# Row sums of three narrow attentions taken from the value products, with masks and a partition shuffle to join the halves

## Chip, cores and metric

One core of one Trainium2 chip. The metric is the device time of one execution, in microseconds (us); the kernel is launched once.

## What is computed

Two layers on x of 8 batches x 256 tokens x 256 features, each a self-attention, a cross-attention and a feed-forward part, with a layer norm after each. Three of these parts are attentions with 16 heads of 16 features ("narrow"), and they alone are changed:

```python
# L0x: cross-attention to 77 context rows; q and k normalized per head, rotary embedding on q
attn = softmax(einsum('bhqd,bhkd->bhqk', q, k)); o = einsum('bhqk,bhkd->bhqd', attn, v)
# L1x: cross-attention to the same 77 rows, scale 0.25
# L1s: self-attention over 256 tokens inside the last part, after an rms norm
ctx = einsum('bhst,bthd->bshd', softmax(scores), v);  X = X + ctx @ wo
```

A softmax row is exp(s - max) divided by its row sum; the kernel divides after the product with the values.

## The kernel before

The program runs seven stages one after the other: L0a (attention with heads of 64), L0x, the expert choice, L1a, L1x, L1s, the mixture of experts. L0x and L1x come from `context_stage`, L1s from `narrow_stage`. Each engine runs its own list of instructions in a hand-written order; semaphores join them.

The three narrow stages have one shape. A batch b has four steps st, numbered through as n = 4b + st, 32 in all; a step covers four heads, one in each 32-row group of TensorE. For each step:

- TensorE computes scores (queries on partitions) in two pairs of heads into `psS`; VectorE takes the negative row maxima of each pair (`row_max`) into `top`; TensorE transposes them (item "top"), and VectorE adds them to the queries (`shift`).
- TensorE computes the turned products (keys on partitions, maxima already subtracted) in two halves into `psK`; ScalarE takes the exponentials of each half into `pT`. Each half of the turned products is issued beside scores of a later step (`turned_beside_scores`): half 0 of step n beside pair 1 of step n+1, half 1 beside pair 0 of step n+2.
- TensorE multiplies `pT` with the values (`values`, into `psO[:, 0:S]`) and with ones (`row_sums`, into `psO[:, S:2S]`). A head group has 32 columns, for two heads of 16: even and odd steps use the same group. In `vs` each pair of heads has four places of 16 columns: values, empty, empty, values. The even step multiplies with the first two, the odd one with the last two, so the empty columns (zeros) leave the other head's partitions of `psO` as they are; `ones` has ones in one half and zeros in the other, in the same way.
- After each odd step VectorE divides: `out_norm(o)`, o = n // 2, a reciprocal of the sums and a product. ScalarE (`out_high`) and GpSimd (`out_low`) split the result into two parts for the output product (item "out").

TensorE's order in the loop over n: turned half 0, items of slot (st, 0), values of step n-1, item "top" of n+1, turned half 1, row sums of n-1, items of slot (st, 1). Items are projections and transposes for the next batches (q, k, v, qk, xT, kT, qT) and the output product; each takes one of NF banks of `psF` (3 in L0x and L1x, 1 in L1s). A few items "top" in L0x and L1x are preceded by products whose result nobody reads (line 466, `keep_busy`): 1 in L0x at steps 0 and 2 at steps 2, 1 in L1x at steps 0 and, from batch 4 on, at steps 1.

VectorE's order: row_max(n+1, pair 1), what it takes of slot (st, 0), shift(n+1), row_max(n+2, pair 0), at even st `out_norm(n // 2 - 1)`, then other work (in L1s, at st 2, `spread` of the batch before; at st 1 `front_stats`; in L0x at st 2 `join_pairs`). `values` of an even step waits for `o_norm`, since it starts `psO` anew. GpSimd's order in L1s at st 1: `root_front(b+2)`, then `out_low`.

Of the kernel before, what the change touches and what calls it, by code (L numbers as in the profile page):

```python
# [11 lines left out]
F32 = mybir.dt.float32  # L12
# [23 lines left out]
EULER = 2.718281828459045  # L36

# [43 lines left out]
def make_constants(nc, ctx):  # L81
# [6 lines left out]
    sums = nc.dram_tensor("moe_sums", [B * S + P, D], F32).ap()  # L88
    zeroed = ctx.enter_context(nc.semaphore("const_zeroed"))
# [18 lines left out]
    return ident, ident_bf, mask_bf, blank, rows, sums, []  # L108


def context_stage(nc, name, kind, consts, x_in, x_out, w, gate_w=None, aff=None):
# [16 lines left out]
    with ExitStack() as ctx:  # L128
# [19 lines left out]
        ones = sb("ones", [P, 2, 2, HD])  # L148
        rinv = sb("rinv", [P, 2, S])
        oN = sb("oN", [P, 2, S])  # L150
# [58 lines left out]
        k_ready, p_exp = sem("k_ready"), sem("p_exp")  # L209
        r_ready, r_inverse, o_norm, o_high, o_low = sem("r_ready"), sem("r_inverse"), sem("o_norm"), sem("o_high"), sem("o_low")  # L210
# [144 lines left out]
        def _(pool):  # L355
# [100 lines left out]
        def _(pe):  # L456
# [165 lines left out]
            def values(n):  # L622
                b, st = divmod(n, NST)
                par = st % 2
                pe.wait_ge(p_exp, 2 * n + 2)
                if par == 0 and n >= 2:
                    pe.wait_ge(o_norm, n // 2)
                wait_taken(pe, ("v", b // 2), 0)
                for j in range(4):
                    pe.matmul(psO[32 * j:32 * j + 32, 0:S],  # L630
                              vs[0:CTX, b, 4 * (st // 2) + j, 2 * par:2 * par + 2, :].rearrange("p a e -> p (a e)"),
                              pT[0:CTX, n % 2, j, :], start=(par == 0), stop=False)

            def row_sums(n):
                par = n % 2
                if n == 0:
                    pe.wait_ge(zeroed, 5)
                for j in range(4):
                    last = pe.matmul(psO[32 * j:32 * j + 32, S:2 * S], ones[0:CTX, par, :, :].rearrange("p a e -> p (a e)"),
                                     pT[0:CTX, n % 2, j, :], start=False, stop=(par == 1))  # L640
                last.then_inc(r_ready, 1)
# [7 lines left out]
            for n in range(N):  # L649
# [9 lines left out]
                if n:  # L659
                    row_sums(n - 1)  # L660
# [3 lines left out]
            row_sums(N - 1)  # L664
# [6 lines left out]
        def _(act):  # L671
            def take(what, b):
# [42 lines left out]
                elif what[0] == "v":  # L715
                    if what[1] == 0:
                        act.wait_ge(zeroed, 3)
# [30 lines left out]
            def exponential(n, half):  # L748
# [3 lines left out]
                act.activation(pT[0:CTX, n % 2, 2 * half:2 * half + 2, :], psK[0:CTX, :, 0:S], ACT.Exp).then_inc(p_exp, 1)  # L752

# [35 lines left out]
            for n in range(N):  # L789
# [11 lines left out]
                if st == 1 and n // NST >= 2:  # L801
                    finish(n // NST - 2)
            out_high(N // 2 - 1)
# [6 lines left out]
        def _(dve):  # L810
# [102 lines left out]
            def row_max(n, pair):  # L913
# [3 lines left out]
                if n == 0:  # L917
                    dve.wait_ge(zeroed, 3)
# [150 lines left out]
def narrow_stage(nc, name, kind, consts, x_in, x_out, w, extra_out=None):  # L1069
# [16 lines left out]
    with ExitStack() as ctx:  # L1086
# [16 lines left out]
        ones = sb("ones", [P, 2, 2, HD])  # L1103
        rinv = sb("rinv", [P, 2, S])
        oN = sb("oN", [P, 2, S])
# [65 lines left out]
        k_ready, p_exp = sem("k_ready"), sem("p_exp")  # L1171
        r_ready, r_inverse, o_norm, o_high, o_low = sem("r_ready"), sem("r_inverse"), sem("o_norm"), sem("o_high"), sem("o_low")
# [112 lines left out]
        def _(pool):  # L1285
# [22 lines left out]
            pool.memset(vs[:, :, :, :, 1:3, :].rearrange("p r t h e d -> p (r t h) (e d)"), 0.0).then_inc(zeroed, 1)  # L1308
            pool.memset(ones[:], 0.0).then_inc(zeroed, 1)
            pool.wait_ge(zeroed, 3)  # L1310
            for r in range(2):
                pool.memset(ones[:, r, r, :], 1.0).then_inc(zeroed, 1)
# [82 lines left out]
        def _(pe):  # L1395
# [143 lines left out]
            def values(n):  # L1539
# [3 lines left out]
                if par == 0 and n >= 2:  # L1543
                    pe.wait_ge(o_norm, n // 2)
                wait_taken(pe, ("kv",) if rope else ("v",), b)
                for kt in range(KT):
                    for j in range(4):
                        h2 = 4 * (st // 2) + j
                        pe.matmul(psO[32 * j:32 * j + 32, 0:S],
                                  vs[0:KP, b % RV, kt, h2, 2 * par:2 * par + 2, :].rearrange("p a e -> p (a e)"),  # L1550
                                  pT[0:KP, n % 2, j, kt * S:(kt + 1) * S], start=(par + kt == 0), stop=False)

            def row_sums(n):
                par = n % 2
                if n == 0:
                    pe.wait_ge(zeroed, 5)
                for kt in range(KT):
                    for j in range(4):
                        last = pe.matmul(psO[32 * j:32 * j + 32, S:2 * S],
                                         ones[0:KP, par, :, :].rearrange("p a e -> p (a e)"),  # L1560
# [1982 lines left out]
```

## Time and profile before

| | us |
|---|---|
| median of 3 runs | 2167.03 (2165.86 to 2175.17) |
| profiled execution, its own time | 2174.54 |
| its span, first to last instruction | 2172.8 |
| TensorE matmul busy | 1866.4 (86%) |
| VectorE busy | 1202.6 (55%) |
| ScalarE busy | 995.1 (46%) |
| GpSimd busy | 677.5 (31%) |
| mean granted TensorE clock | 0.928 of full |

In order of time the stages lie at: L0x to 575 us, its loop from 383 to 557; L1x loop 1382 to 1534; L1s loop 1587 to 1819; the mixture of experts from 1834. Reading the rows: PE is TensorE's matmul, PEld its weight load, DVE VectorE, ACT ScalarE, POOL GpSimd. A name like L1x_psO is a tile of that stage. `[0.88 <-ACT ...]` at the end of a row of the order of time is the idle time of the engine before it and what is taken to have ended it. The granted clock is the share of the full 2.4 GHz that TensorE was given.

### The profile page before, as it was taken

To read this page: it belongs to the slowest core of one execution; us is meant where nothing else is said; L and a number is where in the kernel's file an instruction comes from. 1 tells how busy PE (TensorE), PEld (TensorE's weight loads), DVE (VectorE), ACT (ScalarE), POOL (GpSimd) and SP (SyncE) were. 2 spreads that over 40 slices of the span, in tenths; PEclk is the share of its full clock that TensorE was granted. 3 is DMA by queue.
4 is the path that set the end of the run, shared out by engine and by line. 5 is a ranking of instruction groups with operands and counts; after the bars stand their busy time and mean duration, and the time that the engine had idled before them with its cause. 6 is when DMAs were issued, how large, how long until landed. Compare 5 with 4: busy or idle time off the path is not lost. (4 is left out here: it accounts for less than half of the span.)

```text
span 2172.8 us, 41833 instructions
## 1 busy us (share of the span) xinstructions
PE 1866.4 (86%) x15764; PEld 1453.1 (67%) x15764; DVE 1202.6 (55%) x2996; ACT 995.1 (46%) x2350; POOL 677.5 (31%) x609
## 2 busy tenths in 40 slices
PE   7888875999489999399999995999599896999994
PEld 6676764676278898277777774666366564788884
DVE  3666654666535455245555554466456664447774
ACT  5656542443245454345555552444244342346663
POOL 2333334675332432223333333111101000243443
PEclk9999996998589999699999999899599997999997
DMA  2000002000353522610000001000103102823333
GB/s 65 11 11 21 11 11 71 2 31 11 114 163 107 155 81 46 202 38 1 11 21 11 11 6 44 26 24 18 56 1 109 50 12 94 308 99 52 52 52 100
DMA packets 97870, 125.52 MB, mean 58 GB/s; under 512 B 8554, under 2 KB 84794, under 8 KB 97642
## 3 DMA queue, kind: packets, MB, share of 16 engines
q1 hardware_dynamic: 84378, 105.07, 14.6%
q0 software_dynamic: 13296, 17.77, 4.8%
q8 instruction: 131, 2.15, 0.4%
q14 instruction: 65, 0.53, 0.1%
HBM read 85.02 MB, written 39.89 MB: 57 GB/s over the span
## 5 line engine op out<-in xcount | busy, mean ns | idle before, releaser
L2110 POOL TENSOR_TENSOR L1a_probs<-L1a_probs,L1a_rinv 128x1024 f32<-128x1024 f32 x64 | 121.3, 1895 | 269.2 <-DVE L1a_rinv L2424 269.2
L2107 POOL TENSOR_TENSOR L0a_probs<-L0a_probs,L0a_rinv 128x256 f32<-128x256 f32 (+1 forms) x128 | 103.3, 828 | 189.6 <-DVE L0a_rinv L2424 189.5
L2416 DVE CUSTOM_DVE_ANT_0 L1a_sbias<-L1a_psS,L1a_bias 128x256 f32<-128x256 f32 x256 | 93.2, 421 | 109.2 <-PE L1a_psS L2218 109.2
L2369 ACT ACTIVATE L1a_probs<-L1a_sbias,L1a_nmx 128x256 f32<-128x256 f32 x256 | 126.5, 497 | 40.0 <-DVE L1a_nmx L2416 40.0
L2369 ACT ACTIVATE L0a_probs<-L0a_sbias,L0a_nmx 128x128 f32<-128x128 f32 (+1 forms) x256 | 112.8, 443 | 29.8 <-DVE L0a_nmx L2416 29.8
L3082 POOL DMA_INDIRECT moe_sums<-moe_y,moe_xg x39 | 81.0, 2076 | 136.8 <-DVE moe_y L3381 117.9
L2667 POOL DMA_INDIRECT ec_sums<-ec_yk,ec_token_at x32 | 59.0, 1844 | 190.5 <-ACT ec_yk L2788 185.6
L1643 ACT ACTIVATE L1s_pT<-L1s_psK 128x1024 f32<-128x1024 f32 x64 | 65.6, 1025 | 102.7 <-PE L1s_psK L1516 102.7
L2853 DVE TENSOR_TENSOR ec_h<-ec_sg,ec_psU 128x512 f32<-128x512 f32 x64 | 44.0, 687 | 119.9 <-ACT ec_sg L2775 119.9
L1790 DVE TENSOR_REDUCE L1s_top<-L1s_psS 128x4 f32<-128x1024 f32 x64 | 78.4, 1226 | 48.4 <-PE L1s_psS L1501 48.3
L3160 PE MATMUL moe_psY<-moe_wts,moe_hT 128*128 (+1 forms) x440 | 104.0, 379 | 0.8 <-ACT moe_hT L3227 0.8
L2700 PE MATMUL ec_psG<-ec_xs,ec_wt 128*128 128x512 f32 x384 | 99.3, 394 | 2.1 <-issue 2.1
L2416 DVE CUSTOM_DVE_ANT_0 L0a_sbias<-L0a_psS,L0a_later 128x128 f32<-128x128 f32 (+1 forms) x256 | 76.1, 354 | 43.6 <-PE L0a_psS L2215 43.1
L2700 PE MATMUL ec_psU<-ec_xs,ec_wt 128*128 128x512 f32 x384 | 98.7, 393 | 0.0
L2714 PE MATMUL ec_psA<-ec_wdt,ec_hT 128*128 128x256 f32 x768 | 94.4, 284 | 0.2 <-DVE ec_hT L2812 0.2
L2714 PEld LDWEIGHTS ec_psA<-ec_wdt,ec_hT 128*128 128x128 f32 x768 | 92.8, 192 | 0.5 <-DVE ec_hT L2812 0.4
L3160 PEld LDWEIGHTS moe_psY<-moe_wts,moe_hT 128*128 128x128 f32 x440 | 83.1, 189 | 14.2 <-issue 1.0
L2431 DVE COPY L1a_pT<-L1a_psT 128x1024 f32<-128x1024 f32 x64 | 78.2, 1222 | 20.7 <-PE L1a_psT L2233 20.7
L2700 PEld LDWEIGHTS ec_psG<-ec_xs,ec_wt 128*128 128x128 f32 x384 | 72.7, 191 | 17.3 <-issue 2.4
L2247 PE MATMUL L0a_psO<-L0a_pT,L0a_lat 128*64 128x256 f32 (+1 forms) x512 | 56.9, 342 | 31.8 <-issue 31.6
L2775 ACT ACTIVATE ec_sg<-ec_psG 128x512 f32<-128x512 f32 x64 | 38.2, 597 | 99.1 <-PE ec_psU L2700 99.1
L2700 PEld LDWEIGHTS ec_psU<-ec_xs,ec_wt 128*128 128x128 f32 x384 | 72.9, 190 | 15.4
(527 smaller groups left out, 5016.1 us busy)
## 6 DMA issues: line engine op xcount, KB each, us to landing
ec_wg<-in_L_ffn_w_gate SPq DMA_DIRECT2D x8, 1024.0 KB, 9.4
ec_wu<-in_L_ffn_w_up SPq DMA_DIRECT2D x8, 1024.0 KB, 13.1
ec_wd<-in_L_ffn_w_down SPq DMA_DIRECT2D x8, 1024.0 KB, 6.2
moe_rows<-blank SPq DMA_DIRECT2D x1, 5070.0 KB, 19.2
moe_xg<-moe_rows SPq DMA_DIRECT2D x39, 130.0 KB, 2.1
moe_wts<-in_L_ffn_e_gate SPq DMA_DIRECT2D x8, 512.0 KB, 10.1
moe_wts<-in_L_ffn_e_up SPq DMA_DIRECT2D x8, 512.0 KB, 10.0
moe_wts<-in_L_ffn_e_down SPq DMA_DIRECT2D x8, 512.0 KB, 10.1
```

Of the source, the lines that this page charges most:

```text
L1643: act.activation(pT[0:KP, n % 2, 2 * half:2 * half + 2, :], psK[0:KP, :, 0:KT * S], ACT.Exp).then_inc(p_exp, 1)
L1790: dve.tensor_reduce(top[:, n % 2, :, 64 * pair + HD:64 * pair + 64:32].rearrange("p t j -> p j t"), psS[:, 2 * pair:2 * pair + 2, :].rearr ...
L2107: last = pool.tensor_tensor(v, v, bcast(rinv[:, r, :, t], 2, KEYS[t]), ALU.mult)
L2110: last = pool.tensor_tensor(v, v, bcast(rinv[:, r, :, :].rearrange("p h t -> p (h t)"), 2, S), ALU.mult)
L2369: ins = act.activation(probs[:, r, j, at], sbias[:, g % 2, j, at], ACT.Exp, bias=nmx[:, r, j, t:t + 1], scale=-1.0, accum_out=sums[:, r, j ...
L2416: last = dve.tensor_tensor_reduce(out=sbias[:, g % 2, j, at], in0=psS[:, slot + j, at], in1=added, scale=-1.0, scalar=LARGE, op0=ALU.add, ...
L2431: dve.tensor_copy(pT[:, g % 2, :, :].rearrange("p j (k r c) -> p r (j k) c", r=2, c=64), psT[:, :, 0:PW].rearrange("p r (n c) -> p r n c", ...
L2667: pool.indirect_dma_start(sums, bass.IndirectOffsetOnAxis(ap=token_at[:, s, e:e + 1], axis=0), yk[:, e % 2, s, :], None, compute_op=ALU.add)\
L2700: last = pe.matmul(ps[:, i % 2, :], wt[:, a, j, c, i * P:(i + 1) * P], xs[:, b, c, :], start=(n == 0), stop=(n == len(products) - 1))
L2714: last = pe.matmul(psA[:, half, s % 2 * D:(s % 2 + 1) * D], hT[:, a, i, s * P:(s + 1) * P], wdt[:, b, i, :], start=(i + n == 0), stop=(i = ...
L3082: pool.indirect_dma_start(sums, bass.IndirectOffsetOnAxis(ap=xg[:, j % RX, D:D + 1].bitcast(U32), axis=0), y[:, j % RY, :], None, compute_ ...
L3160: last = pe.matmul(psY[:, 0:D], hT[:, g % 2, f, :], down_weights(e)[:, f * D:(f + 1) * D], start=(f == 0), stop=(f == FC - 1))
```

## The change

`vs` gets ones instead of zeros in its empty columns, so the same product gives in one half of the 32 partitions the values and in the other half the row sums of that head. Since the even and the odd step now both fill all partitions, they go to different halves of `psO`: even to 0:S, odd to S:2S. `row_sums` and the tile `ones` go away. For the even step the values lie on the lower 16 partitions of each group, the sums on the upper 16; for the odd step it is the other way round. To join them, ScalarE copies `psO[:, 0:S]` twice (`out_halves`), with a mask of 0 and 1 per partition as scale (`which_half`), and VectorE adds the other half under the opposite mask. That gives all sums and all values, with the sums of a head 16 partitions away from its values; the reciprocal is taken and shuffled by 16 partitions within each group of 32 (`SWAPPED`). The masks are made once, on VectorE, from the identity matrix.

```diff
+SWAPPED = [*range(16, 32), *range(16)]
 # make_constants: after the GpSimd work
+            dve.wait_ge(made, 5)
+            dve.tensor_reduce(sixteens[:], ident[:].rearrange("p (a e) -> p a e", e=16), AX_X, ALU.add).then_inc(counted, 1)
+            dve.wait_ge(counted, 1)
+            dve.tensor_reduce(which_half[:], sixteens[:].rearrange("p (a h) -> p h a", h=2), AX_X, ALU.add).then_inc(counted, 1)
 # both stages, GpSimd
-            pool.memset(vs[:, :, :, 1:3, :], 0.0).then_inc(zeroed, 1)
-            pool.memset(ones[:], 0.0).then_inc(zeroed, 1)
-            pool.wait_ge(zeroed, 3)
-            for r in range(2):
-                pool.memset(ones[:, r, r, :], 1.0).then_inc(zeroed, 1)
+            pool.memset(vs[:, :, :, 1:3, :], 1.0).then_inc(zeroed, 1)
 # TensorE
                 if par == 0 and n >= 2:
-                    pe.wait_ge(o_norm, n // 2)
+                    pe.wait_ge(o_joined, n // 2)
-                    pe.matmul(psO[32 * j:32 * j + 32, 0:S],
+                    last = pe.matmul(psO[32 * j:32 * j + 32, par * S:(par + 1) * S],
...
-            def row_sums(n):
...
                 turned_beside_scores(n, 1)
-                if n:
-                    row_sums(n - 1)
 # ScalarE
+            def out_halves(o):
+                act.wait_ge(r_ready, 2 * o + 2)
+                if o >= 2:
+                    act.wait_ge(o_joined, o - 1)
+                act.activation(half_sums[:, o % 2, :], psO[:, 0:S], ACT.Copy, scale=which_half[:, 1:2])
+                act.activation(half_values[:, o % 2, :], psO[:, 0:S], ACT.Copy, scale=which_half[:, 0:1]).then_inc(o_halved, 1)
...
                 if st % 2 == 1 and n >= 3:
                     out_high(n // 2 - 1)
+                if st % 2 == 0 and n >= 2:
+                    out_halves(n // 2 - 1)
                 exponential(n, 1)
 # VectorE
             def out_norm(o):
-                dve.wait_ge(r_ready, 2 * o + 2)
-                dve.reciprocal(rinv[:, o % 2, :], psO[:, S:2 * S]).then_inc(r_inverse, 1)
-                dve.wait_ge(r_inverse, o + 1)
+                dve.wait_ge(o_halved, o + 1)
                 if o >= 2:
                     dve.wait_ge(o_low, o - 1)
-                dve.tensor_tensor(oN[:, o % 2, :], psO[:, 0:S], rinv[:, o % 2, :], ALU.mult).then_inc(o_norm, 1)
+                dve.scalar_tensor_tensor(out=all_sums[:, o % 2, :], in0=psO[:, S:2 * S], scalar=which_half[:, 0:1],
+                                         in1=half_sums[:, o % 2, :], op0=ALU.mult, op1=ALU.add).then_inc(o_joined_sums, 1)
+                dve.scalar_tensor_tensor(out=all_values[:, o % 2, :], in0=psO[:, S:2 * S], scalar=which_half[:, 1:2],
+                                         in1=half_values[:, o % 2, :], op0=ALU.mult, op1=ALU.add).then_inc(o_joined, 1)
+                dve.wait_ge(o_joined_sums, o + 1)
+                dve.reciprocal(rinv[:, o % 2, :], all_sums[:, o % 2, :]).then_inc(r_inverse, 1)
+                dve.wait_ge(r_inverse, o + 1)
+                dve.stream_shuffle(rinv_there[:, o % 2, :], rinv[:, o % 2, :], SWAPPED).then_inc(r_moved, 1)
+                dve.wait_ge(r_moved, o + 1)
+                dve.wait_ge(o_joined, o + 1)
+                dve.tensor_tensor(oN[:, o % 2, :], all_values[:, o % 2, :], rinv_there[:, o % 2, :], ALU.mult).then_inc(o_norm, 1)
```

`r_ready` now counts value products instead of row sums, so the exponential that overwrites `pT` is released one block earlier. The products of `keep_busy` stay as they are.

## Rows read from the trace of the kernel before

**Rows 1.** Stretches: us, PE, PEld, DVE, ACT, POOL busy, granted clock, DMA share, GB/s.

```profile
383.00:557.00 174.00, 164.67 (x1718) 111.76 (x1720) 108.04 (x222) 74.44 (x149) 109.14 (x92) 0.91 0.05 15
1382.00:1534.00 152.00, 147.47 (x1630) 97.18 (x1628) 88.48 (x179) 67.81 (x132) 24.54 (x29) 0.93 0.05 17
1587.00:1819.00 232.00, 212.28 (x2540) 140.21 (x2532) 152.12 (x243) 97.84 (x135) 19.70 (x28) 0.99 0.14 43
```

**Rows 2.** Costliest groups, TensorE's row sums: busy us, mean ns of one, idle before.

```profile
L639 PE MATMUL L1x_psO<-L1x_pT,L1x_ones 77*32 77x256 f32 x256 | 22.2, 421 | 0.0
L1559 PE MATMUL L1s_psO<-L1s_pT,L1s_ones 128*32 128x256 f32 x512 | 34.9, 391 | 0.0
```

**Rows 3.** The same view: operations of 256 columns on VectorE and ScalarE.

```profile
L935 DVE TENSOR_TENSOR L1x_oN<-L1x_psO,L1x_rinv 128x256 f32<-128x256 f32 x16 | 6.8, 424 | 0.6
L1832 DVE SCALAR_TENSOR_TENSOR L1s_xn<-L1s_y,L1s_rstd,L1s_norm 128x256 f32<-128x256 f32 x16 | 7.5, 507 | 1.6 <-POOL L1s_rstd L1327 1.6
L689 ACT ACTIVATE L0x_qc<-L0x_psF 128x256 f32<-128x256 f32 x16 | 6.2, 385 | 22.3 <-PE L0x_psF L461 22.3
```

**Rows 4.** L1x, batch 4, order of time: start, us, engine, line, operation.

```profile
1455.88 0.34 PE L588 MATMUL L1x_psS<-L1x_keys,L1x_qs 32*128 32x77 f32 x2
1456.49 0.64 PE L639 MATMUL L1x_psO<-L1x_pT,L1x_ones 77*32 77x256 f32 x8
1457.19 1.76 DVE L931 RECIPROCAL L1x_rinv<-L1x_psO 128x256 f32<-128x256 f32 x1
1459.33 0.47 DVE L919 TENSOR_REDUCE L1x_top<-L1x_psS 128x4 f32<-128x308 f32 x1
1459.51 0.64 PE L630 MATMUL L1x_psO<-L1x_pT,L1x_vs 77*32 77x256 f32 x8 [0.88 <-ACT L1x_pT L752]
1460.62 0.38 PE L563 MATMUL L1x_psF<-ident,L1x_top 128*128 128x128 f32 x2
...
1465.45 0.34 PE L588 MATMUL L1x_psS<-L1x_keys,L1x_qs 32*128 32x77 f32 x2
...
1469.65 0.44 PE L563 MATMUL L1x_psF<-ident,L1x_top 128*128 128x128 f32 x2
```

**Rows 5.** L1s, one batch, after step 2, order of time.

```profile
1722.38 0.48 PE L1501 MATMUL L1s_psS<-L1s_qk 32*128 32x256 f32 x2
1723.45 1.07 PE L1559 MATMUL L1s_psO<-L1s_pT,L1s_ones 128*32 128x256 f32 x16
1724.45 1.70 PE L1400 MATMUL L1s_psF<-L1s_xT,L1s_wqk 128*128 128x256 f32 x12
...
1728.95 1.23 DVE L1790 TENSOR_REDUCE L1s_top<-L1s_psS 128x4 f32<-128x1024 f32 x1
1730.33 0.41 PE L1482 MATMUL L1s_psF<-ident,L1s_top 128*128 128x128 f32 x2 [0.47 <-DVE L1s_top L1790]
```

**Rows 6.** Who waited for whom, L0x, 400 to 540 us: total, times, longest.

```profile
PE L0x_psF L563 <- DVE L0x_top L919: 1.8, 4, 0.5
```

**Rows 7.** L1s, order of time: item "out" after step 1, turned products after step 3.

```profile
1719.41 1.67 PE L1400 MATMUL L1s_psF<-L1s_wo,L1s_oT 128*128 128x256 f32 x12 [0.66 <-issue]
...
1733.07 0.48 PE L1501 MATMUL L1s_psS<-L1s_qk 32*128 32x256 f32 x2 [0.26 <-ACT L1s_pT L1643]
```

**Rows 8.** End of L1x, order of time.

```profile
1534.61 1.76 DVE L931 RECIPROCAL L1x_rinv<-L1x_psO 128x256 f32<-128x256 f32 x1 [3.06 <-PE L1x_psO L639]
```

**Rows 9.** Shorter stretches of L1x, columns as in rows 1.

```profile
1389.50:1393.00 3.50, 2.61 (x43) 1.42 (x36) 2.41 (x5) 1.88 (x4) 1.82 (x2) 1.00 0.00 0
1393.00:1396.50 3.50, 3.50 (x26) 2.79 (x30) 0.48 (x1) 1.10 (x4) 0.14 (x1) 0.52 0.02 5
1510.00:1514.00 4.00, 3.77 (x54) 2.35 (x55) 2.71 (x9) 1.66 (x3) 1.20 (x2) 1.00 0.01 4
1513.80:1534.00 20.20, 18.71 (x130) 9.29 (x130) 8.49 (x17) 5.48 (x10) 3.09 (x4) 0.55 0.04 14
1457.50:1461.00 3.50, 2.62 (x33) 1.69 (x31) 2.27 (x3) 1.48 (x3) 0.95 (x2) 1.00 0.03 7
```

More of the change, by code:

```diff
@@ L107, in _ @@
             pool.wait_ge(made, 5)
-    return ident, ident_bf, mask_bf, blank, rows, sums, []
+        @block.vector
+        def _(dve):
+            dve.wait_ge(made, 5)
+            dve.tensor_reduce(sixteens[:], ident[:].rearrange("p (a e) -> p a e", e=16), AX_X, ALU.add).then_inc(counted, 1)
+            dve.wait_ge(counted, 1)
+            dve.tensor_reduce(which_half[:], sixteens[:].rearrange("p (a h) -> p h a", h=2), AX_X, ALU.add).then_inc(counted, 1)
+            dve.wait_ge(counted, 2)
+    return ident, ident_bf, mask_bf, blank, rows, sums, [], which_half
 def context_stage(nc, name, kind, consts, x_in, x_out, w, gate_w=None, aff=None):
@@ L209, in context_stage @@
         k_ready, p_exp = sem("k_ready"), sem("p_exp")
+        o_halved, o_joined_sums, o_joined, r_moved = (sem(k) for k in ("o_halved", "o_joined_sums", "o_joined", "r_moved"))
         r_ready, r_inverse, o_norm, o_high, o_low = sem("r_ready"), sem("r_inverse"), sem("o_norm"), sem("o_high"), sem("o_low")
@@ L626, in values @@
                 if par == 0 and n >= 2:
-                    pe.wait_ge(o_norm, n // 2)
+                    pe.wait_ge(o_joined, n // 2)
                 wait_taken(pe, ("v", b // 2), 0)
                 for j in range(4):
-                    pe.matmul(psO[32 * j:32 * j + 32, 0:S],
-                              vs[0:CTX, b, 4 * (st // 2) + j, 2 * par:2 * par + 2, :].rearrange("p a e -> p (a e)"),
-                              pT[0:CTX, n % 2, j, :], start=(par == 0), stop=False)
-            def row_sums(n):
[L635 to L640, printed above, removed]
+                    last = pe.matmul(psO[32 * j:32 * j + 32, par * S:(par + 1) * S],
+                                     vs[0:CTX, b, 4 * (st // 2) + j, 2 * par:2 * par + 2, :].rearrange("p a e -> p (a e)"),
+                                     pT[0:CTX, n % 2, j, :], start=True, stop=True)
                 last.then_inc(r_ready, 1)
@@ L1307, in _ @@
             pool.memset(top[:], 0.0).then_inc(zeroed, 1)
[L1308 to L1312, printed above, removed]
+            pool.memset(vs[:, :, :, :, 1:3, :].rearrange("p r t h e d -> p (r t h) (e d)"), 1.0).then_inc(zeroed, 1)
             def residual(b):
@@ L1548, in values @@
                         h2 = 4 * (st // 2) + j
[L1549 to L1560, printed above, removed]
-                                         pT[0:KP, n % 2, j, kt * S:(kt + 1) * S], start=False,
-                                         stop=(par == 1 and kt == KT - 1))
+                        last = pe.matmul(psO[32 * j:32 * j + 32, par * S:(par + 1) * S],
+                                         vs[0:KP, b % RV, kt, h2, 2 * par:2 * par + 2, :].rearrange("p a e -> p (a e)"),
+                                         pT[0:KP, n % 2, j, kt * S:(kt + 1) * S], start=(kt == 0), stop=(kt == KT - 1))
                 last.then_inc(r_ready, 1)
@@ L1676, in _ @@
                     out_high(n // 2 - 1)
+                if st % 2 == 0 and n >= 2:
+                    out_halves(n // 2 - 1)
                 exponential(n, 1)
@@ L1682, in _ @@
                     scale_x(b + 2)
+            out_halves(N // 2 - 1)
             out_high(N // 2 - 1)
```

55 lines of the change are left out of this document (40 added, 15 removed).

## The prediction, made before the changed kernel was built or run

> **What bounds the kernel now.** I read the granted clock and the stage sums first, then the costliest groups, then one batch of each stage in order of time, then what ended the waits. The change touches three of the seven stages: L0x, L1x and L1s, 174, 152 and 232 us long, in which TensorE is busy 95%, 97% and 92% of the time and VectorE 62%, 58% and 66% [rows 1]. So TensorE looks like the bound, and the products that go away stand there as 22.2 us in L1x, as much again in L0x, and 34.9 us in L1s [rows 2], 79 us together. That would be the answer of the busy shares. The order of time says otherwise. In each step one chain runs across the engines: the second half of the turned products of step n stands beside scores of step n+2; VectorE takes their maxima (row_max), then, in every even step, joins and normalizes (out_norm), then takes the maxima of the other pair; only then can TensorE transpose them (item "top"), and everything behind "top" waits in TensorE's queue. I call the time from the start of these turned products to the next "top" an interval; with the 0.36 us from "top" to the next turned products the intervals add up to the stage. In an odd step TensorE fills the interval. In an even one VectorE's chain is nearly as long as TensorE's work: in L1x, after step 0, TensorE already waits 0.88 us ahead of the value products (the view names the exponential, but out_norm's product, 0.42 us from 1458.99 on, ended last) and the interval is 4.74 us; after step 2 it is 4.20 us [rows 4]. In L1s the interval after step 2 is 7.95 us, VectorE works through it without a gap, and "top" waits for the maxima [rows 5].
>
> **Row sums removed.** A block of them takes 0.64 us in L1x, of which the next item covers 0.07, so 0.57 from start to start (twice that, 1.0, at half clock), and 1.00 us in L1s [rows 4, 5]. That is the most that an interval can give back. An interval bound by TensorE gives all of it.
>
> **Joining added on VectorE.** Before: reciprocal 1.76 and product 0.42 [rows 3, 4]. After: two scalar_tensor_tensor from PSUM, the reciprocal, a shuffle, the product. The trace has no such form with PSUM and no shuffle. Nearest rows, all 128x256: product from PSUM 0.42, scalar_tensor_tensor in SBUF 0.51 [rows 3]. Independent operations overlap a little: from the reciprocal's start to the next maxima are 2.14 us, less than the 1.76 + 0.42 of the two [rows 4]. I take 0.33 + 0.33 + 0.42 = 1.1 us; the bounds are 0.7 (a reciprocal that is cheaper from SBUF, a short shuffle) and 1.6 (all at 0.51 without overlap). The Trainium skill (VectorE: DVE Perf Modes, the tier table) gives the shuffle at the pace of a plain one-per-cycle operation, about 0.3 us for 256 elements as an estimate; by that the joining would be 1.0 us.
>
> **ScalarE's two copies.** Each some 0.39 us by a copy of 256 elements from PSUM [rows 3], so 0.8 us, after the value products of the odd step and ahead of the next exponential. Behind the value products TensorE still does "top" (0.36) and the turned products (1.07 in L1s [rows 5], 0.6 in the others), so ScalarE is done about 0.2 us before it is needed; queued behind the copies is that exponential, and for it waits the next half of the turned products. VectorE's wait for the copies ends before its maxima do. I cost this at nothing inside the loop; without that cover it is up to 0.8 us in 48 even steps, of which at most a third, 13 us, would show.
>
> **PSUM free earlier.** The even value products now wait for the joining and not for the normalized output, 1.3 us earlier: the wait of 0.88 us [rows 4] moves from the value products to "top", because the same VectorE is still late there.
>
> **The sum, at the present clock.** L1x: after steps 1 and 3 TensorE bounds, 13 x 0.57 = 7.4 back; last batch, at half clock [rows 9], 4 x 1.0 = 4.0 back. After step 2, 4.20 becomes 1.31 (to the reciprocal) + 2.14 + 1.1 + 0.48 + 0.1 = 5.13, so 0.93 lost, 7 times: 6.5. After step 0, read in the same way in the other batches: the three with a v item are long on TensorE and give 1.3 together, batch 2 loses 0.8, batches 4 and 6, as in [rows 4], 0.4 each; 0.3 lost. L0x: 17 intervals bound by TensorE, 9.7 back, and 4.0 in the last two batches at half clock; after step 2 of batches 1, 3, 5, 7, without a v item, "top" waits for the maxima already (4 times, up to 0.5 us [rows 6]): 3.8 lost. L1s: after step 3 the turned products wait for the exponential and not for TensorE (0.26 us even with the row sums in front): nothing back. After step 1 item "out" waits for out_low, which GpSimd holds behind root_front, fed by VectorE (0.66 us) [rows 7]: nothing back in batches 1 to 5. After step 0 0.45 of the 1.0 is left; after step 2 the 1.1 goes straight onto the interval. So +0.65 in five batches, -2.0 in batch 0, -0.4 in batch 6: +0.8. Tails: at the end of each stage the reciprocal started behind the last row sums [rows 8]; now two copies (0.8), the two joins and the shuffle stand in the chain for one block of sums: +1.2 each, 3.6. The constants: a wait of VectorE and two small reductions in the first block, +0.5. Together -7.4 - 4.0 + 6.5 + 0.3 - 9.7 - 4.0 + 3.8 + 0.8 + 3.6 + 0.5 = -9.6 us. With 0.7 or 1.6 us for the joining, and some 25 intervals in which it shows: -20 or +3.
>
> **The clock.** This is what I take to decide. Less work and more waiting makes TensorE thinner, and in these stages the granted clock already falls when it is. In L1x between 1389.5 and 1393.0 TensorE was busy 2.61 of 3.5 us, and in the next 3.5 us the clock was 0.52, that is 1.2 GHz for nearly all of it; with 2.62 of 3.5 busy at 1457.5 it didn't fall; after 1510 to 1514, 3.77 of 4 busy but with no large item, it fell and stayed low (0.55 over the last 20 us) [rows 9]. The new idle stretches ahead of "top" are longer than any of these: 1.5 to 2 us in L1x (5.13 less TensorE's own 4.20 - 0.57 = 3.6 or 4.74 - 0.88 - 0.57 = 3.3 [rows 4]), 2.2 in L0x, 2.5 in L1s, and no row sums on either side of them. I count 10 in L1x, 4 in L0x, 6 in L1s. Rows bound the outcome between no fall (the 2.62 row) and one each. I take half. One fall costs at most 1.7 us, since 3.5 us at 0.52 do the work of 1.8 at full clock [rows 9]; I take 1.5, the idle stretches absorbing the rest. In L1x, where few large items follow, I take two spells each. 5 x 3.0 + 2 x 1.5 + 3 x 1.5 = 22.5 us.
>
> The profiled execution was 2174.5 us (span 2172.8), the median is 2167.0; I put differences onto the median. 2167.0 - 9.6 + 22.5 = 2179.9, so **2180 us**.
>
> **Rivals.** (a) The clock holds. For it: the 2.62 of 3.5 us at full clock, and L1s at 0.99 though 8% idle [rows 1, 9]. Against: two falls after shorter waits. Then 2167.0 - 9.6 = 2157. The Trainium skill (TensorE: Matmul & The Clock Gate, HAM oscillation) names long gaps of idleness as what halves the clock; by that rule none of the new stretches would be long enough, which is this rival. The trace disagrees in part: both falls came after stretches in which TensorE waited for under 1 us in all [rows 9]. (b) **Slower side:** L1x and a part of L0x drop and stay at half clock, as the last 20 us of L1x do, since it recovers only where large items stand close. If half of the 125 us of TensorE work left in L1x (147.5 - 22.2 [rows 1, 2]) runs at 1.75 times, and a fifth of L0x's 143: 47 + 21, less 10 that the idle stretches absorb: 2167 - 10 + 58 = 2215. It decides from the point where a fall in L1x isn't made good within its batch. (c) VectorE is cheap or its chain not the bound: the joining adds 0.5 us or less, TensorE bounds nearly everywhere, the clock holds: some 25 exposed intervals give 0.6 us more each, 2157 - 15 = 2142. Against it: VectorE's unbroken row in L1s. (d) The busy-share answer, all 79 us or the 68 from start to start: 2099. Two fifths of the intervals are bound elsewhere, so I give it 1 in 100.
>
> **Chances.** The forecast 0.49 (2168 to 2195, by a quarter or all of the falls), (a) 0.24 (2150 to 2164), (b) 0.17, (c) 0.09, (d) 0.01. The range reaches from the middle of (a) and the edge of (c) to (b): 2151 to 2216. A measurement can tell about 0.5%, 10.8 us, from no change: faster is under 2156.2, slower over 2177.8. (c), (d) and a third of (a): 0.17 faster; two thirds of (a) and a third of the forecast: 0.32 same; the rest 0.51 slower.
>
> **What the new profile would show.** Right: no L639 and L1559 groups; the interval after step 2 in L1x near 5.1 us with "top" released by the maxima, those after odd steps near 3.6; VectorE 17 to 20 us busier in each of the three stages; the granted clock of L1x well under 0.93, with several dips inside the batches. Wrong: a clock as before would make it (a); an idle stretch ahead of "top" under 1 us after step 2 would make it (c); an exponential that starts late behind the copies would put the 13 us of ScalarE back in. What would break the forecast altogether is a shuffle of over 1 us, or a free TensorE that pulls the next items forward so that the idle stretches close.

## The result, and the profile after

The changed kernel takes 2231.4 us in the median (2226.6 to 2235.3), the kernel before 2170.2 on the same chip: 1.028 of it, 95% interval 1.024 to 1.032. It is slower, by 61 us, where I had forecast 13. It lies above the whole range. The profiled executions have spans of 2227.1 and 2172.8 us, so 54 us are to be found.

Stretches of the changed kernel, columns as in rows 1: first the loops of L0x, L1x and L1s, then the last 50 us of L1x.

```profile
384.50:560.50 176.00, 152.08 (x1463) 111.04 (x1462) 125.27 (x283) 86.90 (x180) 109.53 (x92) 0.87 0.05 15
1386.50:1564.50 178.00, 163.41 (x1371) 115.17 (x1370) 106.38 (x239) 80.56 (x161) 24.48 (x29) 0.71 0.05 15
1618.50:1868.50 250.00, 200.31 (x2029) 137.68 (x2028) 169.02 (x303) 111.15 (x166) 19.46 (x28) 0.89 0.13 39
1516.00:1566.00 50.00, 45.07 (x290) 28.68 (x288) 26.21 (x61) 18.16 (x37) 6.72 (x8) 0.50 0.03 11
```

From the first value product of a stage to its last L0x is 2 us longer, L1x 27, L1s 18. The rest is 7 us, of which 4 lie behind L1s's last value product: some 1.5 in the tail of L1s, the others in the mixture of experts, which the change doesn't touch. (From that product to the end most kernels took 355 to 359 us, and those on the chip of e1 to e4 376 to 382, whatever the attentions did.) In L1x TensorE is busy 16 us longer than in [rows 1] although the row sums are gone: its granted clock fell from 0.93 to 0.71, and for the last 50 us it is at 1.2 GHz throughout. In L1s the clock fell from 0.99 to 0.89.

L1x, batch 3, after step 2, in order of time (start, us, engine, line, operation; in brackets the idle time ahead of it and what ended it), the answer to [rows 4]:

```profile
1456.08 0.47 ACT L761 ACTIVATE L1x_half_sums<-L1x_psO,which_half 128x256 f32<-128x256 f32 x1 [0.17 <-PE L1x_psO L644]
1456.31 0.34 PE L602 MATMUL L1x_psS<-L1x_keys,L1x_qs 32*128 32x77 f32 x2
1456.45 0.47 ACT L762 ACTIVATE L1x_half_values<-L1x_psO,which_half 128x256 f32<-128x256 f32 x1
...
1457.03 0.59 ACT L755 ACTIVATE L1x_pT<-L1x_psK 77x512 f32<-77x512 f32 x1
1457.09 0.48 DVE L932 TENSOR_REDUCE L1x_top<-L1x_psS 128x4 f32<-128x308 f32 x1 [0.25 <-PE L1x_psS L602]
1457.49 0.47 DVE L946 SCALAR_TENSOR_TENSOR L1x_all_sums<-L1x_psO,which_half,L1x_half_sums 128x256 f32<-128x256 f32 x1
...
1457.88 0.47 DVE L948 SCALAR_TENSOR_TENSOR L1x_all_values<-L1x_psO,which_half,L1x_half_values 128x256 f32<-128x256 f32 x1
...
1458.27 1.74 DVE L951 RECIPROCAL L1x_rinv<-L1x_all_sums 128x256 f32<-128x256 f32 x1
...
1460.05 0.43 DVE L953 STREAM_SHUFFLE L1x_rinv_there<-L1x_rinv 128x256 f32<-128x256 f32 x1
1460.52 0.42 DVE L956 TENSOR_TENSOR L1x_oN<-L1x_all_values,L1x_rinv_there 128x256 f32<-128x256 f32 x1
1460.86 0.47 DVE L932 TENSOR_REDUCE L1x_top<-L1x_psS 128x4 f32<-128x308 f32 x1
...
1461.48 0.41 PE L577 MATMUL L1x_psF<-ident,L1x_top 128*128 128x128 f32 x2 [1.52 <-DVE L1x_top L932]
...
1462.43 1.55 PE L475 MATMUL L1x_psF<-L1x_xT,L1x_wqk 128*128 128x256 f32 x6
```

VectorE goes from the maxima at 1457.09 to those at 1460.86 without a gap: 3.77 us. TensorE waits 1.52 us ahead of "top". The interval is 1461.48 - 1456.31 = 5.17 us; I had worked out 5.13. What I had not sized is the last line: the six products of the next item take 1.55 us, against 0.97 for the same item at full clock. Two stretches of the same place, the interval and the 3.5 us behind it:

```profile
1456.31:1461.50 5.19, 3.67 (x46) 2.78 (x45) 4.76 (x10) 2.69 (x6) 0.03 (x1) 1.00 0.41 106
1461.50:1465.00 3.50, 3.50 (x33) 2.88 (x33) 1.07 (x3) 1.07 (x2) 0.70 (x1) 0.65 0.00 0
```

The clock was full while TensorE waited, and fell right behind the wait. L1s, step 2, the answer to [rows 5]: 1769.38 - 1760.17 = 9.21 us where it was 7.95, with 2.75 us of waiting in place of 0.47, and the products behind it (0.80 for 0.48) at half clock:

```profile
1760.17 0.48 PE L1524 MATMUL L1s_psS<-L1s_qk 32*128 32x256 f32 x2
...
1769.38 0.41 PE L1505 MATMUL L1s_psF<-ident,L1s_top 128*128 128x128 f32 x2 [2.75 <-DVE L1s_top L1809]
...
1769.72 0.80 PE L1524 MATMUL L1s_psS<-L1s_qk 32*128 32x256 f32 x2
```

### The profile page after: what moved, and what is told of

Same layout as the page of the kernel before. It is cut to its first block and busy times, and to the rows that moved or that the text cites. A ratio compares the mean times of both kernels' runs of the same rounds, so it can differ in the third digit from the quotient of the medians.

```text
span 2227.1 us, 40157 instructions
## 1 busy us (share of the span) xinstructions
PE 1858.6 (83%) x14740; PEld 1469.2 (66%) x14740; DVE 1259.4 (57%) x3190; ACT 1036.0 (47%) x2446; POOL 674.5 (30%) x600
## 5 line engine op out<-in xcount | busy, mean ns | idle before, releaser
L1524 PE MATMUL L1s_psS<-L1s_qk 32*128 32x256 f32 x512 | 85.7, 465 | 11.3 <-ACT L1s_pT L1652 11.3
L1539 PE MATMUL L1s_psK<-L1s_qk 32*128 32x256 f32 x512 | 87.4, 466 | 1.3 <-ACT L1s_pT L1652 1.2
```

The source lines that it names most:

```text
L1524: last = pe.matmul(psS[:, j, t * KEYS:(t + 1) * KEYS], qk[r, b % 2, st, t * P:(t + 1) * P], qk[r, b % 2, st, S:QK], start=True, stop=True)
L1539: last = pe.matmul(psK[0:KP, jj, kt * S:(kt + 1) * S], qk[r, b % 2, st, S + kt * KP:S + (kt + 1) * KP], qk[r, b % 2, st, 0:S], start=True, ...
```

## The experiments

My theory (A): VectorE's longer chain makes TensorE wait ahead of "top", after such a wait the clock halves, and this, not the chain itself, is most of the loss. Rivals: the chain alone (B, G), the thinner TensorE alone (C), ScalarE's copies, and that both halves of the change are needed. Each ratio is to the kernel before on the same chip, in brackets its 95% interval. Stages are one profiled execution each, from the first value product to the last; counted so, the kernel before has 173.3, 150.7 and 231.2 us, 555.2 together ("the loops" below). The profiled execution took 6, 10 and 15 us more than the median of its kernel for e1, e5 and e12, and 5 and 6 less for e2 and e8, so a few us in a stage mean nothing. The ratios come from all executions.

| kernel | ratio | L0x us, clock | L1x us, clock | L1s us, clock |
|---|---|---|---|---|
| before | 1 | 173.3, 0.91 | 150.7, 0.93 | 231.2, 0.99 |
| changed | 1.028 (1.024, 1.032) | 175.4, 0.87 | 177.4, 0.71 | 249.4, 0.89 |
| e1, changed, waits filled | 1.010 (1.007, 1.012) | 172.9, 0.95 | 152.6, 0.96 | 243.0, 0.96 |
| e2, before without row sums | 0.991 (0.989, 0.993) | 158.8, 0.94 | 137.4, 0.94 | 227.7, 0.94 |
| e3, joining and row sums | 1.052 (1.049, 1.054) | 195.0, 0.88 | 199.6, 0.76 | 253.2, 0.97 |
| e4, before, last batch of L1x filled | 1.003 (1.000, 1.006) | 173.4, 0.91 | 147.5, 0.99 | 231.6, 0.99 |
| e5, before, VectorE's joining added | 1.029 (1.021, 1.037) | 190.7, 0.86 | 191.7, 0.73 | 244.3, 0.97 |
| e6, changed without the copies | 1.025 (1.017, 1.032) | 175.8, 0.86 | 183.3, 0.67 | 245.5, 0.91 |
| e7, shuffle and product moved | 0.994 (0.990, 0.997) | 168.5, 0.88 | 136.0, 0.95 | 233.4, 0.91 |
| e8, e7 with a little filling | 0.994 (0.991, 0.997) | 167.7, 0.90 | 133.6, 1.00 | 230.9, 0.96 |
| e9, only the product moved | 1.009 (1.006, 1.011) | 168.4, 0.90 | 155.7, 0.84 | 249.3, 0.85 |
| e10, before, product moved | 1.008 (1.005, 1.010) | 176.7, 0.90 | 151.3, 0.94 | 243.4, 0.97 |
| e11, e7 filled at fewer places | 0.992 (0.989, 0.995) | 167.9, 0.88 | 142.8, 0.90 | 231.2, 0.96 |
| e12, changed, one filler per wait | 1.008 (1.006, 1.010) | 182.1, 0.84 | 152.5, 0.93 | 245.3, 0.93 |

### e1: the waits filled

```diff
-item(("top",), n + 1, (1, 0, 2, 0)[st] if rope else (1, 1 if n >= 4 * NST else 0, 0, 0)[st])
+item(("top",), n + 1, (1, 2, 2, 3)[st] if rope else (1, 3 + (1 if n >= 4 * NST else 0), 0, 4)[st])
 # narrow_stage
+item(what, b, 3 if what[0] == "out" else 0)
+item(("top",), n + 1, 5 if n % NST == 3 else 0)
```

> The changed kernel with TensorE kept at work where it waits in even steps: products of 256 columns whose result nobody reads, put ahead of the item that waits: in L1x 3 more ahead of 'top' after an odd step's index 1 and 4 after index 3, in L0x 2 and 3, in L1s 5 ahead of 'top' at index 3 and 3 ahead of item 'out'. VectorE's and ScalarE's work is as in the changed kernel. Theory A (the time went to TensorE's clock, which falls after these waits and stays low): granted clock of L1x back from 0.71 to 0.90 or more and L1x from 178 to about 155 us, L1s from 250 to 234, L0x 176 to 172; the whole some 2180 to 2190 us against 2231. Rival B (VectorE's longer chain alone sets the stages): clock rises but L1x stays at 174 us or more, the whole at 2220 or above.

The stretches of its three loops, columns as above:

```profile
381.40:554.30 172.90, 158.62 (x1537) 117.64 (x1536) 123.73 (x280) 86.72 (x179) 109.07 (x92) 0.95 0.05 15
1382.80:1535.40 152.60, 147.43 (x1473) 108.30 (x1474) 105.33 (x239) 80.48 (x161) 24.60 (x29) 0.96 0.06 17
1591.80:1834.70 242.90, 211.71 (x2137) 150.75 (x2140) 168.40 (x302) 110.70 (x165) 19.29 (x28) 0.96 0.13 41
```

VectorE's and ScalarE's work is the same within 1.6 us in each stage, TensorE has some 280 matmul records more, and the loops are 602.3 - 568.5 = 33.8 us shorter, 24.8 of them in L1x. With more work and an unchanged chain a stage can only get shorter by TensorE's speed, so some 34 of the 47 us that the change added to the three stages came back with the clock. By the ratios it is 39 of 61; 1.010 of 2170 us is 2191, at the edge of what I expected. The 34 is no exact price of the clock: the fillers cost time where they outlast the wait, and they also brought back low clock that the kernel before has (L0x at 0.95 for its 0.91). B falls for L1x. In L1s I expected 234 and got 243. The chain is a part of that (9.58 for 8.32 us from "top" to "top" after step 2), fillers that outlast their wait and 10.5 us for 6.4 after step 1 of the last batch, at a clock of 0.67, are others.

### e2 and e3: each half of the change alone

```diff
 # e2, on the kernel before: row_sums() and its calls out, r_ready after the values
-dve.reciprocal(rinv[:, o % 2, :], psO[:, S:2 * S])
+dve.reciprocal(rinv[:, o % 2, :], fixed[:])
 # e3, on the changed kernel: values() and row_sums() as before, and
-act.activation(half_sums[:, o % 2, :], psO[:, 0:S], ACT.Copy, scale=which_half[:, 1:2])
+act.activation(half_sums[:, o % 2, :], psO[:, S:2 * S], ACT.Copy, scale=which_half[:, 1:2])
 # ... all_values is joined from psO[:, 0:S], and the product takes rinv, not rinv_there
```

> The kernel before with the row-sum products taken out and nothing else: the reciprocal reads a constant in SBUF, so the output lacks the division by the sums (that part of the computation is left out). VectorE's chain keeps its length, TensorE gets thinner. Theory A (long waits ahead of 'top' make the clock fall, and both halves of the change are needed for them): L1x about 142 to 148 us at clock 0.9, L1s 228 to 232, the whole 2150 to 2160. Rival C (thinner TensorE alone drops the clock, whatever the chain): L1x 165 us or more at a clock under 0.8, the whole 2200 or more.

> The other half: the changed kernel's two copies on ScalarE and its five operations on VectorE, but values and row sums as in the kernel before, so TensorE's work is that of before and only the chain is longer. Theory A (both are needed): in L1x the interval after step 2 is 5.1 us as in the changed kernel, the odd ones 4.2; the wait ahead of 'top' is 0.5 to 1.0 us, so the clock mostly holds at 0.9: L1x 160 us, L1s 242, the whole about 2195. Rival D (the longer chain alone does it all): L1x at a clock of 0.75 or under and 178 us or more, the whole 2225 or more.

The stretches of L1x and L1s in e2:

```profile
1367.40:1504.80 137.40, 126.31 (x1368) 90.45 (x1370) 86.97 (x179) 67.78 (x131) 24.59 (x29) 0.94 0.06 19
1555.90:1783.50 227.60, 190.82 (x2025) 132.47 (x2028) 150.86 (x243) 98.15 (x135) 19.54 (x28) 0.94 0.14 45
```

e2: without the row sums, and with the old chain, the loops are 31.3 us shorter at clocks of 0.94, although TensorE is as thin as in the changed kernel. C falls: in L1x no wait ahead of "top" is over 0.7 us. In L1s the thinner TensorE does cost some clock, 0.94 for 0.99, and there it also waits longer, 1.47 us ahead of "top" after step 2 for 0.47. e3 went far beyond all that I had written: the loops take 92.6 us more than before, twice the changed kernel's 47. That the lengthened chain needs the thinner TensorE to do harm was wrong. But e3 wasn't clean, either. ScalarE in its L1x, in order of time:

```profile
1434.13 0.48 ACT L777 ACTIVATE L1x_half_sums<-L1x_psO,which_half 128x256 f32<-128x256 f32 x1 [2.44 <-PE L1x_psO L658]
1434.50 0.47 ACT L778 ACTIVATE L1x_half_values<-L1x_psO,which_half 128x256 f32<-128x256 f32 x1
1434.85 0.59 ACT L771 ACTIVATE L1x_pT<-L1x_psK 77x512 f32<-77x512 f32 x1
```

The copies wait 2.44 us for the row sums (L658), which TensorE issues behind the turned products, and the exponential of these turned products stands queued behind the copies.

### e4: the tail of L1x in the kernel before

```diff
-item(("top",), n + 1, ... (1, 1 if n >= 4 * NST else 0, 0, 0)[st])
+item(("top",), n + 1, ... (1, 1 if n >= 4 * NST else 0, 0, 0)[st] + 2 * (n >= 7 * NST))
```

> The kernel before with two more products of 256 columns that nobody reads ahead of each 'top' of the last batch of L1x, where its granted clock was 0.50 to 0.65 for the last 20 us. If large products hold the clock there, that stretch is at 0.9 or more and L1x is 4 to 8 us shorter (whole 2160 to 2163); if the clock there is set otherwise, the fillers cost 8 times 0.4 us at half speed, and L1x is 3 to 6 us longer.

The loop of L1x is 3.2 us shorter and its clock 0.99 for 0.93, so more products of 256 columns do hold it there; I had expected 4 to 8 us, and a gain of the whole isn't seen (1.003, interval 1.000 to 1.006).

### e5 and e6: VectorE's part and ScalarE's part

```diff
 # e5, on the kernel before; nothing is a tile of zeros, unit of ones
+dve.scalar_tensor_tensor(out=all_sums[...], in0=psO[:, S:2 * S], scalar=unit[:, 0:1], in1=nothing[:], ...)
+dve.scalar_tensor_tensor(out=all_values[...], in0=psO[:, 0:S], scalar=unit[:, 0:1], in1=nothing[:], ...)
+dve.stream_shuffle(rinv_there[:, o % 2, :], rinv[:, o % 2, :], SWAPPED)
 # ... and even value products wait for o_joined, as in the changed kernel
 # e6, on the changed kernel
-act.activation(half_sums[:, o % 2, :], psO[:, 0:S], ...)
-act.activation(half_values[:, o % 2, :], psO[:, 0:S], ...)
```

> The kernel before, row sums and all, with only VectorE's part of the joining added (two operations from PSUM that add a tile of zeros, the shuffle, one product as before), and none of ScalarE's copies. Stages from the first to the last value product were 173.3 (L0x), 150.7 (L1x) and 231.2 us (L1s) before; with the joining and the sums both in, copies included, 195.0, 199.6 and 253.2. Theory F (there the copies stood behind the row sums and held the exponential back): here about 181, 163 and 246, the whole 1.015 to 1.022 of before. Rival G (VectorE's longer chain made all of it): 193 or more, 195 or more, 251 or more, the whole at 1.045 or above.

> The changed kernel without ScalarE's two copies: VectorE adds constants in their place, so half of each joined tile is not the true value (that part of the computation is left out). VectorE's and TensorE's work stay. If the copies are hidden, as the prediction costed them, the stages are as in the changed kernel within 3 us each (175.4, 177.4, 249.5), the whole within 0.3% of its 1.028. If the exponential that is queued behind them comes late, L1s and L1x are 6 us or more shorter each and the whole is at 1.020 or less.

e5, the stretches of L0x and L1x and one item "top" of L1x:

```profile
384.60:575.30 190.70, 174.54 (x1711) 118.19 (x1714) 125.58 (x280) 74.42 (x149) 109.06 (x92) 0.86 0.04 14
1401.50:1593.20 191.70, 181.96 (x1617) 118.59 (x1620) 107.38 (x239) 67.90 (x131) 24.44 (x29) 0.73 0.05 14
```

```profile
1460.63 0.41 PE L572 MATMUL L1x_psF<-ident,L1x_top 128*128 128x128 f32 x2 [1.09 <-DVE L1x_top L928]
```

VectorE's joining by itself, with no copies and with every row sum kept, makes the loops 71.5 us longer, not the 35 of theory F. By L0x and L1x rival G was nearer, by L1s (244.3) and the ratio (1.029) theory F. So of e3's 92.6 us some 21 are the queue of copies and the rest the chain; by the ratios, 1.052 and 1.029, the queue has nearly 50. TensorE is busy 95% of L1x, at 0.73: its own work at half clock. L1x is at half clock for 103 us here and for 101 in the changed kernel, but here TensorE still has the row sums to do at that pace. I take this to be why e5 is worse in L0x and L1x; no run separates it. e6: without the copies the loops sum to 604.6 us against 602.3, L1s 4 us shorter, L1x 6 longer at a lower clock; one execution of each can't tell a few us. The copies that the prediction costed at nothing cost nothing beyond these few.

### e7 and e8: the chain shortened

```diff
 # e7, on the changed kernel: out_norm ends with the reciprocal; out_product is the rest
                 if n + 1 < N:
                     row_max(n + 1, 1)
+                if st % 2 == 1 and n >= 3:
+                    out_product(n // 2 - 1)
 # e8: and (1, 1, 2, 1) fillers in L0x, one more at steps 1 and 3 in L1x, 2 and 2 in L1s
```

> The changed kernel with the shuffle and the product moved one step on in VectorE's order, from behind the reciprocal to behind the next maxima, where VectorE only waits for 'top': 0.86 us of the 1.26 leave the chain, nothing else changes. Theory A (longer waits ahead of 'top', and the clock after them, are the loss): the interval after step 2 in L1x is 4.3 us instead of 5.17, the granted clock of L1x 0.85 or more, stages about 165, 152 and 238 us, the whole 0.995 to 1.003 of before. Rival H (the loss is in the thinner TensorE work or the copies, which stay): L1x at 170 us or more with a clock of 0.75, the whole at 1.02 or above.

> The same with a few products that nobody reads where TensorE still waits: one more ahead of 'top' at step indices 1 and 3 in L0x and L1x, two ahead of 'top' at index 3 and of item 'out' in L1s. Theory A: clocks of 0.93 or more in all three stages, about 162, 145 and 235 us, the whole 0.988 to 0.995 of before, faster than both kernels. If the clock held already without them, the products cost up to 0.4 us each, some 5 us in all, against the version without them.

e7, the loop of L1x, and a step of it in order of time:

```profile
1381.60:1517.60 136.00, 125.32 (x1370) 89.31 (x1370) 103.15 (x239) 79.81 (x161) 24.66 (x29) 0.95 0.06 19
```

```profile
1451.55 0.42 DVE L932 TENSOR_REDUCE L1x_top<-L1x_psS 128x4 f32<-128x308 f32 x1
1451.89 0.44 DVE L955 STREAM_SHUFFLE L1x_rinv_there<-L1x_rinv 128x256 f32<-128x256 f32 x1
1452.11 0.41 PE L577 MATMUL L1x_psF<-ident,L1x_top 128*128 128x128 f32 x2 [0.77 <-DVE L1x_top L932]
1452.36 0.43 DVE L958 TENSOR_TENSOR L1x_oN<-L1x_all_values,L1x_rinv_there 128x256 f32<-128x256 f32 x1
...
1453.05 0.96 PE L475 MATMUL L1x_psF<-L1x_xT,L1x_wqk 128*128 128x256 f32 x6
```

The same instructions as in the changed kernel, two of them later in VectorE's list: 0.86 us leave a chain that repeats 15 times in each stage, at most 39 us, and the loops are 602.3 - 537.9 = 64.4 us shorter. L1x alone gives 41.4. Most of that can't be the chain. The item behind "top" takes 0.96 us, full clock. Both e7 and e8 are faster than both kernels; e8's fillers shorten its loops by 5.7 us in the profiled execution, but the ratios don't tell the two apart.

### e9 to e12: how long a wait

```diff
 # e9: as e7, but the shuffle stays; e12: as e1 with
+(1, 1, 2, 1)[st] if rope else (1, 1 + (1 if n >= 4 * NST else 0), 0, 1)[st]   # and 2 and 2 in L1s
 # e10: the kernel before with
+                if st % 2 == 1 and n >= 3:
+                    out_product(n // 2 - 1)   # its product alone
 # e11: as e7 with (1, 0 if b < 2 else 1, 2, b % 2)[st] in L0x, one at step 3 in L1x, 2 and 2 in L1s
```

> The changed kernel with only the product moved behind the next maxima, not the shuffle: 0.42 us of the chain goes instead of 0.86. In L1x the step after index 3 takes about 5.1 us from 'top' to 'top' (5.54 changed, 4.55 with both moved), and TensorE waits some 1.1 us ahead of 'top' (1.5 and 0.5). Theory A' (a wait of about 1 us is already enough to halve the clock, one of 0.5 is not): granted clock of L1x 0.70 to 0.82, L1x 155 to 170 us, the whole 1.008 to 1.02 of before. If the loss is in proportion to the chain instead, all three stages lie half way: L1x 156, L0x 172, L1s 241, the clock 0.83.

> The changed kernel, its chain untouched, with one product of 256 columns that nobody reads in each wait of L0x and L1x and two or one in L1s: the wait of 1.5 us in L1x becomes 1.1, the steps stay at 5.5 us. Theory A' gives the same clock as the kernel with only the product moved, 0.70 to 0.82, and L1x 160 to 172 us. If any work at all in the wait is enough, L1x is at 0.93 or more and 151 us, as with four such products.

> The kernel before with its own product moved behind the next maxima, row sums and all: 0.42 us of VectorE's chain goes, nothing is removed from TensorE. Where the step is bound by TensorE (all odd ones, and most of L1x) nothing comes back: stages about 171, 149 and 229 us, 0.995 to 0.999 of before. If the reordering alone had made the kernel with both moved fast, this one would be at 0.99 or less.

> Shuffle and product moved as before, the fillers cut to where TensorE still waited: none in the first two batches of L0x, one at index 3 of every other batch, in L1x one at index 3, in L1s two ahead of 'top' at index 3 and of item 'out'. Stages about 165, 133 and 231 us with clocks of 0.93 or more, the whole 0.985 to 0.993 of before, faster than both kernels.

e9's times lie where theory A' put them (L1x 155.7, the whole 1.009; the clock 0.84 for at most 0.82), but they don't prove it: L1x and its clock of 0.84 are also what a loss in proportion to the chain would give (156, 0.83). Against proportion speaks L1s, 249.3 us for its 241, no shorter than in the changed kernel. And A' itself, that a wait of about 1 us is already enough, is wrong: behind the five waits of 1.04 us the clock stayed full, and it fell behind 1.91 and two of the three of 1.28 us. e12 missed A' too and came out as its alternative: its steps stay at 5.5 us, but with a wait of 0.9 instead of 1.5 us L1x takes 152.5 us at a clock of 0.93. Its loops are together 22.4 us shorter than the changed kernel's, with a fraction of e1's products, although L0x is longer (182.1, clock 0.84); by the ratios it is as good as e1. e9 has both outcomes in one stage; two items "top" and the 4 us behind each:

```profile
1446.35 0.41 PE L577 MATMUL L1x_psF<-ident,L1x_top 128*128 128x128 f32 x2 [1.04 <-DVE L1x_top L932]
...
1455.49 0.41 PE L577 MATMUL L1x_psF<-ident,L1x_top 128*128 128x128 f32 x2 [1.28 <-DVE L1x_top L932]
```

```profile
1446.35:1450.35 4.00, 4.00 (x46) 2.94 (x47) 2.70 (x9) 2.92 (x6) 0.73 (x1) 1.00 0.00 0
1455.49:1459.49 4.00, 4.00 (x34) 3.38 (x35) 1.38 (x5) 2.39 (x6) 0.72 (x1) 0.62 0.00 0
```

All items "top" of L1x after the stage's first, in the profiled executions of all fourteen kernels, where TensorE waited 0.4 us or more, with the granted clock of the 4 us behind each (one stood in a stretch at half clock already and is left out):

| wait ahead of "top" | how many | clock under 0.85 behind it |
|---|---|---|
| 0.4 to 1.12 us | 39 | 3 |
| 1.27 to 1.40 us | 14 | 10 |
| 1.5 us and more | 15 | 15 |

Where the wait was shorter than 0.4 us or none, ahead of the last batch, the clock fell behind 1 of 264. The changed kernel has six of the last row, and e7 none but one of 1.40 us, which the clock survived. e3, whose TensorE keeps the row sums, fell behind all five of its waits of 1.27 us. Long waits aren't the only cause: in the last batch of L1x the clock also falls without one, in the kernel before and in e2. And the table is no rule for other places. Counted in the same way, the clock fell behind 13 of 17 waits of 1.5 us and more in L0x and behind 56 of 66 in L1s, and behind 9 of 35 and 5 of 124 of those up to 1.12 us.

e10 was a miss that teaches something. Moving the product in the kernel before makes it slower, 1.008, with 12 us in L1s:

```profile
1733.55 0.41 DVE L1813 TENSOR_TENSOR L1s_oN<-L1s_psO,L1s_rinv 128x256 f32<-128x256 f32 x1
...
1734.07 1.07 PE L1554 MATMUL L1s_psO<-L1s_pT,L1s_vs 128*32 128x256 f32 x16 [1.24 <-issue]
```

There the product reads `psO` itself, so the next even value products wait for it, 1.24 us here. In the loop of L1s TensorE waits 12.1 us ahead of value products, in eight places, where the kernel before waits 2.1. In the changed kernel the joining operations have freed `psO` long before. So the order of e7 pays only together with the change: the change needs the reordering, and the reordering needs the change.

e11 is the fastest in the ratios by a hair (0.992), no more than e7 and e8 within the intervals. Its profiled L1x had one long spell of half clock: 142.8 us for e8's 133.6. It began at 1365.6 us, behind the stage's first "top", where e8 has one of 3.5 us, and here it lasted to 1403.2, into batch 1. e11 has one filler less per batch there than e8, but one execution can't say that this is why.

## Why the prediction was wrong

**Right: what bounds the kernel.** The busy shares misled, the intervals held. After step 2 in L1x 5.17 us (forecast 5.13), after odd steps 3.57 (forecast 3.6; turned products at 1452.37, "top" at 1455.94). From "top" to "top" at full clock, the changed kernel against before: after step 2 5.54 for 4.56, after step 0 of batch 4 5.49 for 5.04, after step 1 3.92 for 4.51. That is the forecast's +0.93, +0.4 and -0.57. After step 3 the changed kernel never ran at full clock; e12 took 4.13 for 4.73.

**Right: the prices.** The two joining operations start 0.39 us apart, the shuffle took 0.44, the reciprocal from SBUF 1.74 for 1.76. In L1s the step after step 2 grew by 1.26 us; I took 1.1, within 0.7 to 1.6. The Trainium skill (VectorE: DVE Perf Modes, the tier table) had given the shuffle some 0.3 us as an estimate; it measured 0.44, and the sum of 1.0 us by it is the farther from 1.26. ScalarE's copies at nothing: e6 bears it out within what one execution tells. VectorE busy 17 to 18 us more in each stage, as forecast.

**Partly wrong: the sum at the present clock.** For the three loops it came to -13.7 us. Against the same step of the kernel before, from "top" to "top", the 49 of 93 steps that the changed kernel ran at full clock throughout add up to -0.7 us, so the sum was some 13 us too good. In L0x I had -9.9 from the intervals; but after step 0 the chain bounds there too (5.49 to 5.68 for 5.33 us), and after step 2 it takes 1.12 more (6.21 for 5.09): of the 5.9 us that I expected beside the last two batches at most 2 came, and of the 4.0 in the last two nothing (37.1 us for 37.0 from the second "top" of batch 6 to the last). The 4.0 us of L1x's last batch didn't come either, since its half clock began a batch earlier. In L1s I had +0.8 us with the reading "+0.65 per batch"; at full clock it is +1.27 - 0.34 = +0.93.

**Wrong: the clock.** The step that failed is the size of this term, 22.5 us: "I take half", and 1.5 us for a spell, two spells in L1x and one elsewhere. The other 44 of the 93 steps, those touched by half clock, are 50 us longer than in the kernel before: 25 in L1x where I had 15, 19.5 in L1s where I had 4.5, 5.6 in L0x where I had 3. (Some us of this are the longer chain in those same steps; filling the waits gave 34 us back in the loops, 24.8, 6.5 and 2.6 of them in these stages.) I counted 20 waits and let half of them end in half clock. After each stage's first "top" there were 17 of 1.5 us or more, and 16 were followed by it: 6 of 6 in L1x, 7 of 7 in L1s, 3 of 4 in L0x. And the spells were longer: a mean clock of 0.71 over 177 us is about 0.58 x 177 = 103 us at half clock in L1x, where the kernel before has 21; that is some 17 per fall, 54 of them in one piece at the end. In L1s the step behind the long wait, 6.27 us before, took 7.3 to 8.9 after step 3 of batches 1 to 5, 8.3 us more together, and the last batch lost more. I had weighed two rows of falls against one without, and drew the coin between them. The row without, 2.62 of 3.5 us busy [rows 9], had a wait of 0.88 us; the new waits were to be 1.5 and more by my own sum. Of 39 waits of up to 1.12 us 36 left the clock alone, so that row spoke for waits of its own length and for no longer ones.

**The rivals.** (b) named the right mechanism and its point, "where a fall isn't made good within its batch", and got 0.17: L1x did drop and stay, from 1510 us on, where its last batches have few large items. Its 2215 came near partly by luck: it put 58 us of clock into L1x and L0x, where the steps show some 31, left out L1s with its 20, and took off 10 us by the sum, which didn't come. (a), that the clock holds, fell, and with it the rule of the Trainium skill (TensorE: Matmul & The Clock Gate, HAM oscillation) that asks for long gaps: the runs disagree, in L1x a wait of 1.5 us or more was enough 15 times of 15. (c) was about e7: with 0.86 us off the chain the kernel does come out faster, at 0.994. (d) is far off: the -0.7 us at full clock stand against its -68 to -79.

**Taken together**, the 54 us of the profiled executions are 47 in the loops and 7 outside. From the first "top" of each stage to the last it is 49.4 us: -0.7 in steps at full clock and +50.1 in those with half clock in them. What e1's fillers gave back, 34 us in the loops and 39 by the ratios, is the part that experiment shows; the remaining 13 are e1's surplus products, the longer chain and what stays of low clock. How these 13 divide isn't settled.

## What to carry to other kernels

An engine that waits now and then can still be the one whose clock matters: before lengthening a chain that ends in front of TensorE, work out the new wait and look in the trace for what the clock did behind waits of that length, not of shorter ones. When work moves from TensorE to another engine's chain, place the added operations behind the point where TensorE is released; here 0.86 us in another place was worth 64 us in the loops. And ask which buffer each operation holds: a like move, e10's, loses where it keeps the accumulators occupied.

## What the runs showed of the hardware

- Longer spells than expected: L1x of the changed kernel was at half clock for 101 us in six spells, the last of 54 us, in which TensorE was busy 45.07 of 50. So a busy TensorE alone did not bring the clock back there. In the kernel before, two products of 128 x 256 more ahead of each "top" of the last batch (e4) took the clock of L1x from 0.93 to 0.99. Whether their size, their number or shorter waits do it, no run separates.
- Adding work made the stages shorter: one product of 256 columns more in each wait (two in L1s) took 22.4 us off the changed kernel's loops.
- Removing TensorE's row sums alone kept the clock of L1x at 0.94 with TensorE busy 92%, while 95% busy in e5's L1x had 0.73. The busy share said nothing of the clock here, and it can't: the same products take longer at half clock (1.55 us for 0.97) and so raise it. The longest waits told more: 0.7 us at most in e2's L1x, up to 2.1 in e5's.
